# A score mask moved from TensorE to VectorE, and an output addition moved to GpSimd, in a windowed attention

## The reference, cut to what matters

```python
q = layernorm(x); k = v = ctx_1024           # 16 heads of 16 channels
scores = einsum('bhcid,bhcjd->bhcij', q_c, k_c)
band = abs(j - w - i) <= w                   # w = 128
scores = where(band & in_range, scores, big_neg)
out = softmax(scores) @ v_c
x = x + tanh(g_xattn[0]) * out
```

## Time and profile before

| | us |
|---|---|
| median of 3 runs | 762.05 (761.35 to 763.06) |
| profiled execution, first to last instruction | 764.1 |
| TensorE busy | 709.2 |
| VectorE busy | 367.9 |
| ScalarE busy | 316.1 |
| GpSimd busy | 346.0 |

### The profile page before, as it was taken

How to read it: one execution, slowest core, us unless ns; L and a number is a source line. 1 busy time by engine, 2 the same in 40 slices (tenths; PEclk the granted TensorE clock), 3 DMA queues, 4 the chain that set the end, 5 groups by cost and what they waited for, 6 DMA issues and landing times.

```text
span 764.1 us, 16259 instructions
## 1 busy us (share of the span) xinstructions
PE 709.2 (93%) x5308; PEld 589.9 (77%) x5315; DVE 367.9 (48%) x1102; ACT 316.1 (41%) x850; POOL 346.0 (45%) x475
## 2 busy tenths in 40 slices
PE   4889999988999999998899988999999999999994
PEld 2457666665758999997666646999999999999993
DVE  3568777887656645534898774122122121221210
ACT  3336666665544432330566523332332322323321
POOL 6333333333016655442478634554544545545422
PEclk9999999999989999999999999999999999999998
DMA  6975666545867999923344448557433623446211
GB/s 206 183 172 105 127 123 125 121 100 103 259 198 270 374 371 373 361 84 123 43 77 74 114 138 265 138 160 211 118 101 60 164 47 63 110 100 172 38 17 14
DMA packets 146935, 114.67 MB, mean 150 GB/s; under 512 B 50562, under 2 KB 138285, under 8 KB 146859
## 3 DMA queue, kind: packets, MB, share of 16 engines
q1 hardware_dynamic: 136586, 100.59, 48.4%
q0 software_dynamic: 10272, 13.13, 8.2%
HBM read 153.02 MB, written 24.40 MB: 232 GB/s over the span
## 4 chain that ended last, share of the span: by engine, by line
PE 44%; DVE 5%; POOL 1%; issue 1%; DMA 1%; ACT 0%; SPq 0%; POOLq 0%; DVEq 0%
PE e_HP L1201 18%; PE e_Y L1213 17%; PE c_DN L2037 2%; PE e_T L1188 1%; PE c_U L2004 1%; DVE rows_sb L2233 1%; PE c_AT L2020 1%; PE c_DN L904 1%; PE e_HP L904 1%; PE c_QT L2011 0%; DVE c_st L2217 0%; PE c_DN L2039 0%; PE c_U L2057 0%; DMA c_rb<-L_ffn_router_b_in 0%; DMA out<-e_yo,d_table 0%
## 5 line engine op out<-in xcount | busy, mean ns | idle before, releaser
L1236 ACT ACTIVATE w_down<-e_HP,e_col 128x128 f32<-128x128 f32 x312 | 89.1, 369 | 184.6 <-PE e_HP L1201 171.4
L1201 PEld LDWEIGHTS e_HP<-e_rT,w_up 128*128 128x128 f32 x1248 | 145.4, 192 | 3.1 <-DVE e_rT L1248 1.1
L1201 PE MATMUL e_HP<-e_rT,w_up 128*128 128x128 f32 x1248 | 146.0, 275 | 0.9 <-DVE e_rT L1248 0.9
L1213 PE MATMUL e_Y<-w_down 128*128 128x256 f32 x624 | 141.0, 379 | 0.0
L1213 PEld LDWEIGHTS e_Y<-w_down 128*128 128x128 f32 x624 | 115.6, 190 | 14.1
L1258 DVE TENSOR_TENSOR e_yo<-e_Y,e_b2b 128x256 f32<-128x256 f32 x39 | 16.6, 425 | 216.0 <-PE e_Y L1213 216.0
L1293 POOL DMA_INDIRECT out<-e_yo,d_table x39 | 63.1, 1617 | 124.3 <-DVE e_yo L1261 110.6
L527 DVE TENSOR_REDUCE a_nm<-S 128x2 f32<-128x512 f32 x128 | 83.3, 683 | 32.4 <-PE S L643 31.9
L383 ACT ACTIVATE a_pexp<-S 128x1024 f32<-128x1024 f32 x64 | 64.9, 1017 | 32.7 <-PE S L661 32.3
L1016 PEld LDWEIGHTS e_HP<-e_rT,w_up 128*128 128x128 f32 x512 | 59.5, 192 | 2.2 <-DVE e_rT L1072 1.5
L1016 PE MATMUL e_HP<-e_rT,w_up 128*128 128x128 f32 x512 | 60.0, 275 | 1.0 <-DVE e_rT L1072 1.0
(11 more groups left out here) (346 smaller groups left out, 1201.4 us busy)
## 6 DMA issues: line engine op xcount, KB each, us to landing
w_up<-L_ffn_w_in SPq DMA_DIRECT2D x39, 1024.0 KB
w_down<-L_ffn_w_in SPq DMA_DIRECT2D x39, 1024.0 KB
w_up<-L_ffn_W_in SPq DMA_DIRECT2D x16, 1024.0 KB, 9.3
w_down<-L_ffn_W_in SPq DMA_DIRECT2D x16, 1024.0 KB, 11.8
e_b2b<-L_ffn_b_in SPq DMA_DIRECT2D x55, 128.0 KB, 3.8
scr<-a_parts SPq DMA_DIRECT2D x51, 128.0 KB
a_q<-scr SPq DMA_DIRECT2D x17, 192.0 KB, 3.9
a_k<-scr SPq DMA_DIRECT2D x17, 192.0 KB, 4.4
```

The lines of the kernel that those rows point to most:

```text
L1201: i = e.matmul(HP[r][:, j, :], w1[:, n % WR, k, P * j:P * j + P], rT[:, r, k, :], start=(k == 0), stop=(k == 1))
L1213: i = e.matmul(Y[r][:, 0:D], hT[:, r, j, :], w2[:, n % WR, j, :], start=(j == 0), stop=(j == NJ - 1))
L1236: i = e.activation(hT[:, r, j, :], HP[r][:, j, :], ACT.Gelu, bias=col[:, n % 4, j:j + 1])
```

## The change

The first pass's masks are no longer products. The two triangles become planes 0 and 2 of one tile `band`, with zeros between, so that planes 1 and 2 are the mask row of query half 0, and planes 0 and 1 that of half 1. VectorE's one reduction of a head becomes two operations that add the mask, scale by -1 and reduce with minimum, one for each half; each also writes the masked scores back to PSUM. The second pass's masks stay products. `norm` ends after L512; the addition is `add_out` on GpSimd, into two buffers of `on`. It stands in step n for unit n-3, group 0 behind the splitting of the maxima and before `split`, group 1 at the end of the step; the last units' additions stand between the roots of the next layer's statistics. VectorE's steps are all unrolled instead of looped. The other engines keep their loop.

```diff
@@ attention
-        low = sb("low", [P, P], BF16)
-        upp = sb("upp", [P, P], BF16)
+        band = sb("band", [P, 3, P], BF16)
+        upp, low = band[:, 0], band[:, 2]
+        bands = [band[:, 1:3].rearrange("p a t -> p (a t)"), band[:, 0:2].rearrange("p a t -> p (a t)")]
-        on = sb("on", [P, 2, 4 * DH], F32)
+        on = sb("on", [P, 2, 2, 4 * DH], F32)
@@ pool
+            def add_out(m, g):
+                wait(e, s_n, m.times(2, g + 1))
+                c0 = P * m.mod(2) + 4 * DH * g
+                xs = x_sb[:, bass.ds(m.tile(), 2), c0:c0 + 4 * DH]
+                e.tensor_tensor(xs, xs, on[:, g], ALU.add).then_inc(s_xa, 1)
+            e.memset(on[:], 0.0).then_inc(s_xa, 2)
@@ pool, step(n)
+                if (n - 3).valid():
+                    add_out(n - 3, 0)
                 if not first and not (n.reg is None and n.c == 1):
                     for u in n.splits():
                         split(u)
...
+                if (n - 3).valid():
+                    add_out(n - 3, 1)
             over_units(e, step, -2, NU)
@@ pool, behind the steps
-            for g in range(2, len(NORM_GROUPS)):
-                rows_ln.root(e, g)
+            add_out(Unit(NU - 2), 0)
+            rows_ln.root(e, 2)
+            add_out(Unit(NU - 2), 1)
+            rows_ln.root(e, 3)
+            add_out(Unit(NU - 1), 0)
+            add_out(Unit(NU - 1), 1)
+            rows_ln.root(e, 4)
@@ vector, norm
+                wait(e, s_xa, m.times(2, g + 1))
-                e.scalar_tensor_tensor(on[:].rearrange("p c (h d) -> p (c h) d", d=DH),
+                e.scalar_tensor_tensor(on[:, g].rearrange("p c (h d) -> p (c h) d", d=DH),
...
-                e.tensor_tensor(xs, xs, on[:], ALU.add).then_inc(s_xw, 1)
@@ vector, heads
-                    e.tensor_reduce(nm[:, n.mod(2), h, :], S1[h % 2][:], axis=AX.X, op=ALU.max, negate=True
-                                    ).then_inc(s_mx, 1)
+                    for c in range(2):
+                        i = e.tensor_tensor_reduce(S1[h % 2][:, c, :], S1[h % 2][:, c, :], bands[c], -1.0, 3.0e38, ALU.add, ALU.min,
+                                                   nm[:, n.mod(2), h, c:c + 1])
+                    i.then_inc(s_mx, 1)
@@ vector
-            over_units(e, step)
-            e.wait_ge(s_xw, 4 * NU)
+            for n in range(-2, NU + 3):
+                step(Unit(n))
+            e.wait_ge(s_xa, 2 * NU + 2)
@@ tensor, pass1
-                    e.matmul(dst[:, c, :], q6[0:KR, r, h, P * c:P * c + P], k6[0:KR, r, h, :], start=True, stop=True)
-                    o = 1 - c
-                    i = e.matmul(dst[:, c, P * o:P * o + P], ident[:], (low if c == 0 else upp)[:],
-                                 start=False, stop=True, skip_group_check=True)
+                    i = e.matmul(dst[:, c, :], q6[0:KR, r, h, P * c:P * c + P], k6[0:KR, r, h, :], start=True, stop=True)
```

More of the change, by code:

```diff
@@ L153, in attention @@
         s_s2, s_e, s_pv, s_oe, s_ot, s_n = (sem(n) for n in ("s_s2", "s_e", "s_pv", "s_oe", "s_ot", "s_n"))
-        s_xw, s_zr, s_nm = sem("s_xw"), sem("s_zr"), sem("s_nm")
+        s_xw, s_xa, s_zr, s_nm = sem("s_xw"), sem("s_xa"), sem("s_zr"), sem("s_nm")
         lin = K["lin"]
@@ L248, in pool @@
             e.memset(ident[:], 0.0).then_inc(s_cst, 1)
-            e.memset(low[:], 0.0).then_inc(s_cst, 1)
-            e.memset(upp[:], 0.0).then_inc(s_cst, 1)
+            e.memset(band[:], 0.0).then_inc(s_cst, 1)
             e.memset(v32[:], 0.0).then_inc(s_cst, 1)
-            c[0] = 10
-            e.wait_ge(s_cst, 10)
+            c[0] = 9
+            e.wait_ge(s_cst, 9)
             for m in (identf, ident):
@@ L256, in pool @@
                                 pattern=[[-1, P]], channel_multiplier=1).then_inc(s_cst, 1)
-            e.affine_select(out=low[:], in_=low[:], compare_op=ALU.is_ge, fill=NEG, base=0,
+            e.affine_select(out=low, in_=low, compare_op=ALU.is_ge, fill=NEG, base=0,
                             pattern=[[-1, P]], channel_multiplier=1).then_inc(s_cst, 1)
-            e.affine_select(out=upp[:], in_=upp[:], compare_op=ALU.is_ge, fill=NEG, base=0,
+            e.affine_select(out=upp, in_=upp, compare_op=ALU.is_ge, fill=NEG, base=0,
                             pattern=[[1, P]], channel_multiplier=-1).then_inc(s_cst, 1)
@@ L510, in norm @@
                 e.reciprocal(rz[:], tr[:, :, :, DH]).then_inc(s_xw, 1)
-                wait(e, s_xw, m.times(4, 2 * g + 1))
-                e.scalar_tensor_tensor(on[:].rearrange("p c (h d) -> p (c h) d", d=DH),
+                wait(e, s_xw, m.times(2, g + 1))
+                wait(e, s_xa, m.times(2, g + 1))
+                e.scalar_tensor_tensor(on[:, g].rearrange("p c (h d) -> p (c h) d", d=DH),
                                        O[:, 0:S].rearrange("p (a w) -> p a w", w=32)[:, :, 0:DH],
@@ L526, in heads @@
                         wait(e, s_mp, (n - 2).times(4, 4))
-                    e.tensor_reduce(nm[:, n.mod(2), h, :], S1[h % 2][:], axis=AX.X, op=ALU.max, negate=True
-                                    ).then_inc(s_mx, 1)
+                    if n.reg is None and n.c == 0 and h == 0:
+                        e.wait_ge(s_cst, 17)
+                    for c in range(2):
+                        i = e.tensor_tensor_reduce(S1[h % 2][:, c, :], S1[h % 2][:, c, :], bands[c], -1.0, 3.0e38, ALU.add, ALU.min,
+                                                   nm[:, n.mod(2), h, c:c + 1])
+                    i.then_inc(s_mx, 1)
             def step(n):
@@ L571, in step @@
                     route.keep_turned_vector(e, 3)
-                    e.wait_ge(s_xw, 56)
+                    e.wait_ge(s_xa, 30)
                     rows_ln.take(e, EARLY, EARLY + 2)
@@ L578, in rows_ahead @@
                 if c == NU - 5:
-                    e.wait_ge(s_xw, 16)
+                    e.wait_ge(s_xa, 10)
                     rows_ln.take(e, 0, GT)
                 if c == NU - 4:
-                    e.wait_ge(s_xw, 32)
+                    e.wait_ge(s_xa, 18)
                     rows_ln.variances(e, 0)
@@ L594, in rows_ahead @@
                 if c == NU:
-                    e.wait_ge(s_xw, 48)
+                    e.wait_ge(s_xa, 26)
                     rows_ln.take(e, 2 * GT, EARLY)
@@ L612, in tensor @@
         def tensor(e):
-            e.wait_ge(s_cst, 18)
+            e.wait_ge(s_cst, 17)
             def split_transposes(u):
@@ L660, in pass2 @@
                                  start=True, stop=True)
-                        i = e.matmul(S2[u % 2][:, a, c, P * o:P * o + P], ident[:], (low if c == 0 else upp)[:],
+                        i = e.matmul(S2[u % 2][:, a, c, P * o:P * o + P], ident[:], low if c == 0 else upp,
                                      start=False, stop=True, skip_group_check=True)
```

3 lines of the change are left out of this document (removed).

## The result

The changed kernel took 767.65 us in the median (766.47 to 769.15, four executions) beside 761.73 for the kernel before (761.35 to 763.06, four): a ratio of 1.0064 with a 95% interval of 1.0039 to 1.0090, slower by 0.6%. (The ratios of this document are recorded with their intervals and are not the quotient of the two medians, which is 1.0078 here; the two differ by up to 0.15%.) The forecast had been 762.8. The question is where a few us come from.

What follows compares the result with a forecast made beforehand. SP's queue was taken to bound each attention turn. 764.1 + 0.3 + 0.5 - 1.0 + 0.95 = 764.85, less 2.05: 762.8 us, no change that can be told; own range 761.4 to 764.5, 8-in-10 range 759.7 to 774.

Steps and rivals of the forecast that it cites:

- rival A: Attention turns: VectorE becomes the bound above about 0.92 us a head; slower, 771 to 772 at 1.0; chance 0.30.
- SP's queue sets the turn: Attention turn of 8 heads: SP's issues and landing set the pace, 9.58 us, with TensorE waiting for it.
- the +0.5 over the turns: Steady attention turns: head 2 longer on VectorE delays split and SP's write, 11 turns at 0.05 us each.
- TensorE's relief: First-pass masks leave TensorE: 0.96 us a unit, 15.4 over 128 heads, going in steady turns into its wait for SP.
- VectorE's head: Two operations replace one reduction per head: 0.84 us instead of 0.61, ends 0.68 and 1.18; VectorE occupied 8.91 a turn.
- Before the steady run: First heads up to the first steady write: 1.8 us longer on VectorE against masks and additions saved, +0.3 net.
- GpSimd: Token additions moved there: 0.45 us each, two a turn, covered by its idle time before the split.
- The last units: Attention's end: unit 15's masks saved, against a later root and a slower last addition; together -0.05 us.
- The wait for the root: Tail: group 2's root stands behind unit 14's addition, making VectorE's shift +0.9 us later, +0.55 to TensorE's values.
- What unit 15's masks gave back: Last unit: its masks are on TensorE's path, so removing them gives -1.0 us, VectorE permitting.
- Rival C: Attention turns: TensorE's wait grows to about 1.7 us and its clock falls; slower, 771; chance 0.06.
- The other three layers move with the attention's end: Code behind the attention: shifts only with the attention's end, so it has no term of its own in the sum.

Runs made afterwards that it cites:

- the changed one with 64 products: The changed kernel with 64 one-column products added at the head of PE's program, while PE waits for its first tile: 764.12 us, 1.0011 of the kernel before.
- the mask alone with the 64 products: Kernel before with only the mask moved to VectorE, steps written out, plus 64 one-column products heading PE's program: 762.44 us (0.9991); repeated on another chip, 773.42 (0.9994).
- the addition alone: Kernel before with only the addition to the tokens moved to GpSimd; mask products kept, VectorE looped: 764.59 us, 1.0012.
- the mask part with the 64 products and six fillers: Mask on VectorE and 64 products heading PE's program, with six instead of four filler products in the linear attention's last router turns: 771.93 us, 0.9982 of kernel before.

## Why the prediction came out as it did

The forecast was no change that can be told (0.42) before slower (0.40), and slower came. The time was 4.9 above the forecast and outside the forecast's own range of 761.4 to 764.5. That it lies inside the wide range, up to 774, is luck: that range was drawn for rival A, and what made the kernel slower was neither A nor any other rival. Part by part:

- **SP's queue sets the turn: right; the +0.5 over the turns: not seen.** Forecast 9.58, measured 9.50 and 9.52; most of the 0.1 is a landing of 2.46 where the earlier trace rows had 2.57. From the first steady write of parts to the last, eleven turns, it is 109.4 and 109.2 us in the two profiles of the kernel before. In those of the changed one it is 107.7, and 110.8 with the turn of 12.97 in it; with 64 products it is 109.2. So the turns together gained up to 1.7 us or nothing, where the sum had +0.5.
- **TensorE's relief: right in size, nearly right in where it goes.** Busy time from 110 to 140 fell from 28.07 to 25.68, 0.76 a turn (forecast 0.96). Its wait for the DMA of k did not grow to 1.7: it was 0.78, 1.20 and 0.81 in three turns. The rest became waits for VectorE between the heads, as the row of all first-pass products shows: 6.6 of 17.5 us idle, where the kernel before had 1.0 of 9.4 (before, then after).

```profile
L641 PE MATMUL S<-a_k,a_q 96*128 96x256 bf16 x256 | 52.2, 279 | 9.4 <-DMA a_k<-scr 7.2 <-DVE a_nm L527 1.0 <-issue 0.8
```

```profile
L659 PE MATMUL S<-a_k,a_q 96*128 96x256 bf16 x256 | 44.3, 283 | 17.5 <-DMA a_k<-scr 9.0 <-DVE a_nm L543 6.6 <-issue 0.8
```

- **VectorE's head: a size off.** 0.84 forecast, 0.76 measured; the 0.08 for each accumulator read was nothing, and the main operation's pace was 0.38, not 0.34. VectorE occupied 7.9 of the eight heads' 10.11 us instead of the forecast 8.91. Rival A needed 0.92 and is out. The section "Two Vector instructions with no wait between them" of the Trainium skill's page "VectorE: DVE Perf Modes" is right that there are two instructions (256 of each over the run), and the 0.90 worked out from that page's table was too high for a head, since the second one overlaps.
- **Before the steady run: +0.3 forecast, nothing measured.** The write of parts that came at 65.51 before came at 65.45 (the one ahead of it was still 1.4 late, 49.65 instead of 48.20).
- **GpSimd: right.** 0.455 each; SP's write did not move.
- **The last units: -0.05 together, and nothing clear measured; their parts unproven.** From the last write of parts to the attention's end it is 38.7 us in both profiles of the changed kernel and in the second one of the kernel before (the first, with the low clock of the earlier trace rows, has 41.7); in the changed one with 64 products it is 40.4. The wait for the root was 1.03 for the forecast 0.9, and the last hop 0.57 beside 0.4; removing the first changed the time by less than could be seen. What unit 15's masks gave back (-1.0) was not measured apart.
- **Rival C was right as a mechanism, wrong as a rule.** PE's wait for k went over 2 us in one turn of one profile, the clock fell, and the turn took 3.4 us more. It did not come in the second profile of the same kernel. In that turn the last read of k took 5.2 us to land instead of 3.9 to 4.5, with a q8 packet between issue and landing (75, read issued at 73.34, first product at 78.70). That the packet caused it was not tested. A repeat with the packet at the same time landed in 4.4 and kept its clock.
- **The step that failed isn't in the sum at all.** The prediction says "The other three layers move with the attention's end". They did not: the attention's end came 1.6 us earlier in the profile and the span 3.0 later. Of these 4.6 us, 3.4 are the seam (14.76 instead of 11.35 by the table's last column) and 1.4 the stretch at 446. The missing term is the length of PE's program text: it moves the fetches of all code behind it, and one came to lie on the transfer for which all engines wait at the seam. Its price is 1.8 us, or some 3.5 when the clock falls behind it. The 1.4 has no shown cause.

With the fetch moved away the changed kernel measures 1.0011 (0.9990 to 1.0032), and 762.8 over 762.05 is 1.0010. The forecast's sum agrees with that, as would any sum within 1.5 us of it. Of its parts the mask alone with the 64 products comes to 0.9991 and 0.9994, the addition alone to 1.0012. None of these differs from 1 by more than the measurement can tell.

Left open: why the mask kernels' clock also fell at 446 in five of nine profiles (1.4 us) and in none of five without the mask. On the third chip it fell there in none of four profiles; all four, with and without the mask, have a fall between 475 and 490 instead. One and the same kernel, the mask part with 64 products, showed it in one profile and not in the other, so it does not come in every execution. Open is also why the first measurement shows 0.6% where the second shows 0.25%. No tried version is faster than the kernel before beyond its interval; the lowest ratios are 0.9980 (VectorE's program written out, nothing else) and 0.9982 (the mask part with the 64 products and six fillers).

## What to carry to other kernels

Removing instructions from a looped or written-out program moves the fetches of everything behind them. So before a few us are explained by the edited stage, compare the times of the instruction queue's packets in both traces with the transfers that all engines wait for, and run both kernels with some dozens of harmless instructions ahead: if one of the two times moves by as much as their difference, the difference need not be the edit's own. And work taken from an engine that waits for a DMA queue each turn is worth little until the queue's own turn shrinks.

## What was not expected of the hardware

- One fetch of 16 KB of PE's program occupied a DMA engine for 1.4 to 1.7 us (1.0% to 1.2% of 16 engines over windows of 8.5 to 9 us), and a scatter in flight with it landed in 4.0 to 4.4 us instead of 2.4 to 2.5, in four profiles of four (three kernels). The longer the packet took, the later the scatter landed: 1.35, 1.56, 1.70 and 1.74 us for the packet, 4.0, 4.2, 4.3 and 4.4 for the scatter. The section "Instruction fetch mechanics" of the Trainium skill's page "Runtime: NRT & Kernel Launch" calls the cost of crossing a block mostly hidden. Here PE's products ran on through it, but another queue's transfer did not stay clear of it.
- The accumulator read of a reduction (143 ns by its row) starts together with the next operation and adds nothing to the pace of 0.38 us for 256 elements.
- At the seam an idle time of PE of 3.33 to 3.73 us was followed by half clock in three of four profiles, and one of 1.75 to 1.80 in none of ten.
